# Null-key attention: the keys of head pairs 3 to 7 projected two stages earlier and kept in DRAM, and the weighted sums of a step moved into the next step

## The reference

```python
q = split_heads(layernorm(x) @ Wq)               # 16 heads of 64, 4 batches of 256 queries
k, v = split(ctx @ Wkv)                          # ctx: 256 tokens per batch, 256 wide
k = concat([null_k, k]); v = concat([null_v, v]) # one learned key and value ahead of the 256
p = softmax(q @ k.T / 8)                         # 256 x 257 for each head and batch
x = x + layernorm((p @ v) @ Wout)
```

## Time and profile before

| what | us |
|---|---|
| median of 3 runs | 1119.61 (1118.01 to 1120.69) |
| the profiled execution, its own time | 1116.3 |
| its span, first to last instruction | 1114.5 |
| PE busy, share of the span | 979.7, 88% |
| DVE busy | 823.2, 74% |
| ACT busy | 636.2, 57% |
| POOL busy | 426.2, 38% |
| PE's share of the chain that ended last | 64% |
| DVE's and ACT's shares of it | 16% and 9% |

### The profile page before, as it was taken

The page is one execution under the profiler, slowest core; times in us unless marked ns, Lnnn a source line. Parts: engine busy times, 40 slices in busy tenths (PEclk is TensorE's granted clock), DMA queues, the critical chain, the costliest instruction groups (busy, mean ns, idle before and its releaser), DMA issues.

```text
span 1114.5 us, 18229 instructions
## 1 busy us (share of the span) xinstructions
PE 979.7 (88%) x5958; PEld 720.5 (65%) x5958; DVE 823.2 (74%) x1980; ACT 636.2 (57%) x1594; POOL 426.2 (38%) x664
## 2 busy tenths in 40 slices
PE   5688999999759998868999999996899999998587
PEld 4457887888513434746777777775667777777465
DVE  7855898898667881698989988768665667675663
ACT  3373666766317775366797877973144666664121
POOL 8231122111121110235766767767130565654200
PEclk9697999999859998899999999997899999999789
DMA  5530211122052310300000000303000100003000
GB/s 215 139 122 1 76 39 39 39 67 62 20 170 81 98 40 20 152 1 1 1 1 1 1 1 1 151 1 121 1 1 21 57 1 2 1 14 138 1 1 20
DMA packets 32254, 53.55 MB, mean 48 GB/s; under 512 B 4192, under 2 KB 24448, under 8 KB 31008
## 3 DMA queue, kind: packets, MB, share of 16 engines
q1 hardware_dynamic: 29616, 50.03, 13.5%
q10 hardware_dynamic: 2544, 2.36, 0.7%
HBM read 45.33 MB, written 6.88 MB: 47 GB/s over the span
## 4 chain that ended last, share of the span: by engine, by line
PE 64%; DVE 16%; ACT 9%; issue 6%; DMA 2%; POOL 1%; SPq 1%; DVEq 0%; ACTq 0%
PE psum L1733 8%; PE psum L1356 8%; PE psum L1366 7%; ACT region_d L1795 4%; PE psum L2524 3%; PE psum L1763 3%; PE psum L2453 3%; PE psum L412 3%; PE psum L368 2%; DVE region_d L1931 2%; ACT region_c L1812 2%; PE psum L1719 2%; PE psum L2427 2%; PE psum L2469 2%; DVE null_work L2626 2%
## 5 line engine op out<-in xcount | busy, mean ns | idle before, releaser
L1733 PE MATMUL psum<-gated_parts 128*128 128x512 f32 x768 | 191.1, 400 | 18.7 <-DVE region_d L1931 15.1
L1733 PEld LDWEIGHTS psum<-gated_parts 128*128 128x128 f32 x768 | 137.0, 188 | 69.1 <-DVE region_d L1931 36.8
L2024 POOL TENSOR_TENSOR region_d<-region_d 128x256 f32<-128x256 f32 x126 | 94.6, 751 | 93.1 <-DVE region_d L1931 91.0
L1425 ACT ACTIVATE rounds_work<-psum,region_c 128x512 f32<-128x512 f32 x128 | 84.6, 688 | 28.1 <-PE psum L1356 25.9
L802 DVE TENSOR_REDUCE work<-psum 128x1 f32<-128x512 f32 x128 | 81.8, 686 | 22.0 <-PE psum L368 20.3
L1356 PE MATMUL psum<-parts,split 128*128 128x512 f32 x384 | 95.9, 400 | 0.0
L1366 PE MATMUL psum<-parts,split 128*128 128x512 f32 x384 | 93.3, 392 | 0.0
L1547 POOL CAST parts<-rounds_work 128x1024 fp32r<-128x1024 f32 x32 | 33.4, 1043 | 151.9 <-ACT rounds_work L1425 151.9
L1795 ACT ACTIVATE region_d<-psum,gated_work 128x128 f32<-128x128 f32 x256 | 75.9, 447 | 26.8 <-issue 22.2
L1479 DVE TENSOR_TENSOR parts<-rounds_work,parts 128x1024 fp32r<-128x1024 f32 x64 | 76.3, 1220 | 16.9 <-POOL parts L1547 15.9
L1795 ACT ACTIVATE region_d<-psum,ctx 128x128 f32<-128x128 f32 x256 | 73.0, 375 | 25.2 <-PE psum L1733 15.4
(11 more groups left out here) (450 smaller groups left out, 2190.6 us busy)
## 6 DMA issues: line engine op xcount, KB each, us to landing
rounds_work<-cw_rows SPq DMA_DIRECT2D x32, 256.0 KB, 3.4
region_a<-in_l1v SPq DMA_DIRECT2D x8, 512.0 KB, 4.0
region_b_last<-in_l1o SPq DMA_DIRECT2D x1, 4096.0 KB, 12.3
region_a<-in_l2f SPq DMA_DIRECT2D x1, 4096.0 KB, 12.0
region_b_last<-in_l3f_small SPq DMA_DIRECT2D x1, 4096.0 KB, 12.8
region_a<-in_l3f SPq DMA_DIRECT2D x1, 2080.0 KB, 7.4
region_c<-in_l0f SPq DMA_DIRECT2D x1, 2076.0 KB, 12.3
region_c<-in_l3x SPq DMA_DIRECT2D x1, 2048.0 KB, 7.8
```

The costliest lines, as they stand in the source:

```text
L1425: act.activation(H[g % 2][:, f, :], bank[f], ACT.Gelu_apprx_tanh, bias=W("b1")[:, (g % E) * FT + f:(g % E) * FT + f + 1]).then_inc(h_ready ...
L1733: ins = pe.matmul(bank[2 * (n % 2) + c], src[a][:, t * P:(t + 1) * P], weights[b][:, piece(c)], start=m == 0, stop=m == len(PASSES) - 1)
L2024: pool.tensor_tensor(tile[:, 0:2, :], tile[:, 0:2, :], tile[:, 2:4, :], ALU.add).then_inc(k.pool_chain, 1)
```

## The change

1. **Keys ahead.** A new class `NullKeysAhead` projects the keys of pairs 3 to 7 in the `l1x` stage: ten halves (a pair's 512 context columns each), every half in four quarters. A quarter is one fp32 matmul of 256 columns; it takes the context and the weights as they are, not in high and low parts. Eight quarters stand ahead of the layer norm's transposes, 24 between the query projections and the first loop step, one in each of the first eight loop steps. ACT copies each half to SBUF (`copy`), SP stores it to DRAM (`store`), two in each of five turns of its loop, behind the loads of `l1v`. The weights come by one DMA of 1 MB at the start of the rounds.
2. **Keys loaded.** In the null-key stage SP loads a half's 256 KB into `k32[h]` as soon as the low part of the pair before is made. ACT's high part and DVE's low part of these keys now read `k32` in SBUF instead of a bank. The split of their weights on POOL falls away. When the keys of the coming pair are loaded, its four steps make (q0, k0), (v0, k1), (q1), (v1).
3. **Weighted sums a step later.** The PE's order in a step is now: scores, the first projection, the weighted sums of the step before, turns, the other projection. The sums go to bank 7 (the last two to banks 2 and 3), and projections inside the steps have bank 6 alone: each waits until ACT and DVE have read the one before it. ACT has its first projection copy between the two items' exponentials. DVE takes both maxima first, the first low part ahead of the turned copies and the other behind them.
4. **Last pair.** The output matmuls of tiles 4 to 7 stand together in step 3; step 2 has none.

```diff
+class NullKeysAhead:
+    PAIRS = range(3, 8)
+    BANKS = (4, 5, 4, 5, 6, 7, 4, 5, 6, 4)
+    IN_FRONT, AHEAD = 8, 32
+    def quarter(self, pe, j):
+        n, q, c = j // 4, j % 4 // 2, j % 2
+        pair, h = self.PAIRS[n // 2], n % 2
+        if j % 4 == 0 and self.BANKS[n] in self.BANKS[:n]:
+            last = max(m for m in range(n) if self.BANKS[m] == self.BANKS[n])
+            pe.wait_ge(*self.copied.at(last + 1))
+        first = h * HALF + q * HALF // 2
+        ins = pe.matmul(k.bank[self.BANKS[n]][:, q * HALF // 2:(q + 1) * HALF // 2], self.weights[:, c, pair * P:(pair + 1) * P],
+                        k.ctxT[:, c, first:first + HALF // 2], start=c == 0, stop=c == 1)
...
+        if p + 1 in keys.PAIRS:
+            plan = ((("q", 0), ("k", 0)), (("v", 0), ("k", 1)), (("q", 1),), (("v", 1),))
...
     def bank_of(n):
-        return k.bank[1 + n] if n < 2 else k.bank[6 + n % 2]
+        return k.bank[1 + n] if n < 2 else k.bank[6 + n % 2] if n < FIRST else k.bank[6]
...
-                pe.wait_ge(proj_sb, n - 1)
-                if n >= 6 and MADE[n - 2][0] != "v":
-                    pe.wait_ge(*proj_low.at(LOWS[n - 2]))
+                at = HERE.index(n)
+                same = HERE[at - 1 if at > FIRST else at - 2]
+                pe.wait_ge(proj_sb, same + 1)
+                if n >= 6 and MADE[same][0] != "v":
+                    pe.wait_ge(*proj_low.at(LOWS[same]))
...
         def low_projections(n):
-            src = bank_of(n)
+            src = k32[h] if loaded(what, p) else bank_of(n)
```

More of the change, by code:

```diff
@@ L214, in packed_attention @@
     RX = [k.carve(F32, NH * SLOT) for _ in range(2)]
-    if masked:
+    if not masked:
+        keys.place([k.carve(F32, HALF) for _ in range(2)])
+    else:
         k.carve_from(WORK - 5 * T // 2)
@@ L325, in tensor @@
         bank = k.bank
+        if not masked:
+            for j in range(keys.IN_FRONT):
+                keys.quarter(pe, j)
         k.norm.tensor(pe, use, k.xn)
@@ L434, in tensor @@
         else:
+            for j in range(keys.IN_FRONT, keys.AHEAD):
+                keys.quarter(pe, j)
             pe.wait_ge(*rest.at(first_of(3)))
@@ L450, in tensor @@
                     pe.wait_ge(ahead.z_ready, 2)
+                if not masked and s == 0:
+                    pe.wait_ge(*keys.copied.at(keys.HALVES))
                 second_pass(*divmod(s, STEPS))
@@ L455, in tensor @@
                 first_pass(b, PER * u + 1)
+            if not masked and i < keys.QUARTERS - keys.AHEAD:
+                keys.quarter(pe, keys.AHEAD + i)
             if masked and 2 <= i < 6:
@@ L494, in scalar @@
     def scalar(act):
+        if not masked:
+            for n in range(keys.IN_FRONT // 4):
+                keys.copy(act, n)
         k.norm.scalar(act, use, k.xnT)
@@ L510, in scalar @@
             parts, cols = piece(2 * pair + 1)[2:]
+            if not masked and pair == 1:
+                for n in range(2, 5):
+                    keys.copy(act, n)
             for i in range(3):
@@ L517, in scalar @@
                     store(act, q_dram, NH, parts[i], row, cols).then_inc(stored_q[pair].semaphore, 16)
+                if not masked and pair == 1:
+                    keys.copy(act, 5 + i)
         def context_part(n):
@@ L548, in scalar @@
             s = i - LAG
+            if not masked and i % 4 == 3 and i < keys.QUARTERS - keys.AHEAD:
+                keys.copy(act, (keys.AHEAD + i) // 4)
             if not masked and i % SU == 0 and 0 < i <= ALL:
@@ L736, in sync @@
                 k.load_piece(sp, "l1v", v, UNITS * B)
+                for n in range(2 * v - 2, 2 * v):
+                    if 0 <= n < keys.HALVES:
+                        keys.store(sp, n)
         if masked:
@@ L1553, in sync @@
     def sync(sp):
+        sp.wait_ge(k.x_tiles, NT * number)
+        keys.load_weights(sp)
         for s in range(TURNS):
@@ L2405, in null_key_attention @@
     cleared = k.count("experts_cwT_sb", 2)
+    keys_loaded = [k.count(f"packed_{what}_psum", 8 * keys.HALVES) for what in ("k", "q")]
     def tensor(pe):
@@ new lines, in tensor @@
+        pe.wait_ge(nvw_sb, 1)
+        for n in range(STEPS):
+            p, b = divmod(n, B)
+            if n + 1 < STEPS:
+                scores(*divmod(n + 1, B))
+            here = [m for m in MADE_IN[p][b] if m in HERE]
+            for m in here[:1]:
+                project(m)
+            if n > 0:
+                weighted_sums(n - 1)
+            for i in range(2):
+                turn(2 * n + i)
+            for m in here[1:]:
+                project(m)
+            if p + 1 == PAIRS and b != 2:
+                h = b // 2
+                pe.wait_ge(*cleared.at(h + 1))
+                pe.wait_ge(av_sb, B * (PAIRS - 2) + b + 1)
+                for t in range(TPB * b, TPB * (b + 1)) if h == 0 else range(4, 8):
+                    output(t, range(PAIRS - 1))
@@ L2554, in projections @@
             what, p, h = MADE[n]
-            src = bank_of(n)
-            act.wait_ge(proj_psum, n + 1)
+            if loaded(what, p):
+                src = k32[h]
+                act.wait_ge(*keys_loaded[h].at(16 * (p - keys.PAIRS[0] + 1)))
+            else:
+                src = bank_of(n)
+                act.wait_ge(proj_psum, HERE.index(n) + 1)
             if what == "q":
@@ L2700, in split_weights @@
             if n >= UNITS_AHEAD:
-                pool.wait_ge(proj_psum, max(made("v", p - 2, j) for j in range(B)) if what == "v" else
-                             max(made(w, p - 2, h) for w in ("q", "k") for h in range(2)))
+                pool.wait_ge(proj_psum, max(projected("v", p - 2, j) for j in range(B)) if what == "v" else
+                             max(projected(w, p - 2, h) for w in ("q", "k") if not loaded(w, p - 2) for h in range(2)))
             if what == "v":
```

196 lines of the change are left out of this document (126 added, 70 removed).

## The result

| | median us | runs | ratio to before, 95% interval |
|---|---|---|---|
| before, in the first measurement | 1118.81 | 4 | |
| after, in the first measurement | 1138.61 (1126.72 to 1143.93) | 4 | 1.0129 [1.0075, 1.0182] |
| after, built and measured again | 1128.88 (1121.39 to 1140.11) | 8 | 1.0064 [1.0034, 1.0094] |

The account below looks back on a forecast made before the run. PE was taken to bound the null-key stage, with a score loop hidden behind it; +3.3 + 0.2 - 1.0 + 2.0 - 1.2 = +3.3 on 1116.3 gives 1119.6, plus 3.3 for the median: 1122.9 us, range 1116.3 to 1127.0.

Parts of the forecast that it names:

- The null-key stage: The forecast's sum without its `l1x` term: +4.5 us.
- Pairs 1 and 2 in one bank: Null-key stage: chunks wait for the low part that frees their one bank; pair 21.0 against 19.36 us, twice, +3.3.
- Pairs 3 to 6: Null-key stage, keys loaded: PE's saving goes to score loop and DVE; 19.4 against 19.36 us each, +0.2 together.
- pair 7: Null-key stage, made in pair 6's steps without `v`: 18.3 us, -1.0.
- the last: Last pair's own steps: sums wait for turned copies, two tiles' outputs come later; 26.4 against 24.4 us, +2.0.
- Rival 1: Null-key stage: loaded keys' low parts aren't held by POOL; pairs 3 to 6 take 18.4, total 1117.6 us; chance 0.24.
- the hold: Loaded keys' low parts, both inputs in SBUF, end 0.54 us behind a POOL multiply's end; ten low parts concerned.
- Rival 2: PE alone bounds the null-key stage before and after; 1101 us; chance 0.10, including anything between it and rival 1.
- `l1x`, forecast -1.2: Start of `l1x`: quarters hidden in PE's idle time, transposes and first projection at 2.4 GHz; first pass earlier, -1.2 us.
- I take it that it now stays at 2.4 GHz: Start of `l1x`: eight front quarters fill the idle time where the clock was 1.2 GHz; assumed behind the -1.2.
- Rival 3: PE at 1.2 GHz in the quarters of `l1x`; 24 end ten us behind the loads; 1132 us or so; chance 0.10.
- Costed at nothing: ACT's ten copies, DRAM stores, key loads, POOL's lost work and the 1 MB load: together 0 to +1 us.

Follow-up runs that it names:

- low_on_pool: Kernel after, with the low parts of the loaded keys made by GpSimd instead of VectorE; 1119.01 us, ratio 1.0000 to before.
- no_low: Kernel after, with the low parts of the loaded keys left out, so scores use an old low part; 1118.14 us, ratio 0.9978 to before.
- `l1x` part alone: Everything of the change in `l1x` kept, with the null-key stage of kernel before; 1121.98 us, ratio 1.0016 to before.
- no_quarters: Kernel after without quarters and their copies; stores and loads stay, keys of pairs 3 to 7 left out; 1123.92 us, ratio 1.0071 to before.
- pool_and_fill: Kernel after, loaded keys' low parts on GpSimd, plus 64 unused matmuls ahead of the last stage's transposes; 1118.81 us, ratio 0.9997 to before.
- after_fill36: Kernel after plus 36 unused fp32 matmuls of 128 columns ahead of the last stage's transposes; 1135.78 us, ratio 1.0146 to before.

## Why the prediction was wrong, step by step

The range failed on the first measurement, 1138.6. About 10 of its 20 us go with more time at half clock in all stages, stage 0 above all, for which the forecast had no term; the rest is in the repeat too and is gone through here.

- **The null-key stage, forecast +4.5, measured +4.9.** Pairs 1 and 2 in one bank: forecast +3.3, measured +4.2 (21.89 + 21.47 against 19.76 + 19.36). The mechanism and its two waits are as laid out; each pair's is 2.1 instead of 1.65. Pairs 3 to 6: forecast 19.4 each, +0.2; measured 19.31 to 19.33, -0.2. This is no luck: the four steps were laid out as 4.25, 5.4, 5.1 and 4.7, and came at 4.32, 5.26, 5.17 and 4.58. From there to the end: forecast -1.0 for pair 7 and +2.0 for the last, +1.0; measured +0.9, of which 27.18 against 25.19 stands behind the last scores.
- **Rival 1, the low parts aren't held: refuted.** 1273 ns beside 687. Its price was too small: it put pairs 3 to 7 at 5.3 below the forecast, and `low_on_pool` found 7.5. A pair without the hold takes 17.77, not 18.4, since the two steps behind a loaded key's low part take 4.57 and 4.31 where 4.8 and 4.65 were laid out.
- **Rival 2, PE alone bounds: refuted.** PE waits 13.3 us for the exponentials in that stage, and 5.7 even with the hold gone.
- **`l1x`, forecast -1.2: right to the first pass, wrong behind it.** The transposes run at 2.4 GHz, the first pass comes 1.1 earlier, 32 quarters fit ahead of it, and of the eight beside the maxima those at full clock do. The failed step is that the term ended at the first pass. "I take it that it now stays at 2.4 GHz" was checked against the quarters alone; the half-clock stretch that in before lay on DVE's steps was not followed to where it would lie next. What the runs showed in its place: 32.8 us at half clock from the second pass on instead of 13.1, at 0.31 each, is the +6.2 of after. In all the traces of this code it makes +5.5 on average instead of -1.2 (+4.1 without the two long executions), from -2.9 (`no_low`) to +11.5 (`low_on_pool`). By medians the `l1x` part alone costs less than its measurement can tell, 1.8 us with an interval from -1.1 to +4.6.
- **Rival 3 had the half of it.** It put 1.2 GHz on the 24 quarters ahead of the first pass, where the granted clock of after stayed at 1.00; the place was the second pass. Its size, 10 us, is the upper end of what came.
- **The last stage had no term.** It costs 1 to 2.6 us where the clock rises later there.
- **Costed at nothing:** copies, stores and loads stayed hidden; `no_quarters` has all stores and loads, and its rounds (201.3), `l1f` (315.5) and `l1x` (157.2) are not longer.
- **The sum.** In the pair of traces +4.9, +6.2 and +2.3, with -0.9, +0.7 and -0.6 from stage 0, `l1f` and `l2`: 12.6 of the 13.0 between the executions. By medians it was 9.6.

What stays open: why the clock falls and rises when it does. The Trainium skill (TensorE: Matmul & The Clock Gate, "What's actually happening") says that activity releases the clock. Here PE was busy 10.00 of 10.00 us at 0.50 in two stretches running (`low_on_pool`, 348 to 368), so busy time as the profile counts it did not bring the clock back; no run shows what does. That the quarters are what delays the fall is shown by the table; that they lengthen the stretch is not, since `no_low` and `pool_and_fill` had the shortest ones. What in the new null-key stage moved the last stage's rise was not tried.

## What to carry to other kernels

- Work put into an idle stretch of TensorE has a price beyond its own time: it can move a stretch at half clock to another place. Ask which engine is the bound where that stretch lies now, and which where it would lie next. Under the loop steps that VectorE bounds 18 us at half clock cost next to nothing here (18.0 from the first to the second pass in before, 17.4 with quarters and the clock at full for all but 2 to 4 us); in the TensorE-bound part behind them each us cost 0.31, and its matmuls took 1.5 to 1.6 times as long (the rows below).
- Before moving a read from PSUM to SBUF, look at what GpSimd does beside it: the second SBUF input cost more here than the matmuls that it saved, and giving the operation to GpSimd itself took it back.
- Where executions spread by 1%, compare stages inside traces, and each run's time against its time at half clock, before a cause is looked for in the code.

## What the runs showed of the hardware

- TensorE stayed at 1.2 GHz for 37.5 us (31.6 to 69.1 in `low_on_pool`) while it was busy 37.1 of them, and in `after_fill36` for 35.7 us of second pass (336.0 to 371.7) while it was busy 35.2; in the same code in `no_low` for 10 us. The form of work was 48- and 51-row bf16 matmuls and 128x256 f32 ones.
- Two groups of that loop in after, at half clock (333 to 348 us) and at full (354 to 369), mean ns in the second column behind the bar:

```profile
L440 PE MATMUL psum<-work 51*128 51x256 bf16 x28 | 6.7, 410 | 0.0
L470 PE MATMUL psum<-work 128*32 128x256 f32 x48 | 6.5, 634 | 0.3 <-ACT work L629 0.3
...
L470 PE MATMUL psum<-work 128*32 128x256 f32 x80 | 6.4, 391 | 0.0
L440 PE MATMUL psum<-work 51*128 51x256 bf16 x39 | 5.7, 272 | 0.0
```

- Over the whole program a microsecond more at half clock goes with 0.35 us more of time, in before and after alike; in the second pass of `l1x` with 0.31.
- A subtraction of 128x512 with both inputs in SBUF takes 1191 ns on GpSimd, 1273 on VectorE while GpSimd works, and 687 on VectorE with one input in PSUM. With both in SBUF and nothing on GpSimd, a VectorE instruction of that size (L1510) takes 691 to 693.
